# Attention and LoRA kernel: q and k by seven block products, and turned probabilities through device memory

## Chip, cores, metric

One core of one Trainium2 chip. The metric is the device time of one execution in microseconds; the time of a kernel is the median of its runs. TensorE multiplies, VectorE and ScalarE work on tiles in SBUF and PSUM, GpSimd on tiles in SBUF, and SyncE issues most transfers.

## What is computed

Four batches of 512 tokens of width 256. A block of attention (16 heads of 128) with modulated layer norm before it, then a dense layer with 8 LoRA experts, of which each token takes two:

```python
h = layernorm(x) * (1 + ca) + sa
q = h @ (wq_codes * repeat(wq_scales, 32)) + bq      # 256 -> 2048; k and v alike
scores = einsum('bqhd,bkhd->bhqk', q, k) / sqrt(128)
attn = softmax(scores)
out = einsum('bhqk,bkhd->bqhd', attn, v)
x = x + ga * (out @ wo + bo)
h = layernorm(x) * (1 + cb) + sb
x = x + gb * (h @ W.T + lora(h))                     # top 2 of 8 experts
```

All of it is in 32 bits. Each product is made of three matmuls on values split in a high and a low part (hi x hi + hi x lo + lo x hi), so every operand needs a `_hi` and a `_lo` tile: one engine rounds the value, another subtracts (`three`).

## The kernel before

The 2048 features are worked off in 8 pairs of heads (`pair(p)`; the first and the last are written out, the six between are a hardware loop). A pair has 8 steps, s = 0 to 7: one head of one batch, two heads of batch 0, then batch 1, 2, 3. The step's number is n = 8p + s. Every engine has its own program, and the engines meet by counting semaphores; the order on each engine is written out by hand.

TensorE, in step n: scores of step n (4 tiles of 3 matmuls with 512 columns), the weighted values of step n-2 (`weighted`, 12 matmuls of 512), q of step n+1 and k of step n+1 (`project`, 6 of 512 each: two chunks of the input's 256 features), the output projection of step n-2 (`out_project`, 12 of 256), v for step n+1 (`project_v`, 12 of 256). 

VectorE, in step n: v_lo, four row maxima (`maximum`), four 32x32 block transposes of the probabilities (`turn`, into `pB`), the reciprocal of the sums (`inverse`), o_lo, q_lo, k_lo, four additions of the scaled output rows to `y_acc` (`y_add`).

ScalarE: v_hi, four exponentials, o_hi, q_hi, k_hi, four copies of the landed probabilities into `pT_hi` (`prob_high`); it also issues the loads of the next pair's weights in steps 0 to 3. GpSimd: four low parts `pT_lo` (`prob_low`), the products of weight codes and scales (`product`) and the split of weights (`parts`).

A block transpose only turns inside 32x32 blocks; the blocks themselves must change partition. SyncE does that with 16 SBUF to SBUF transfers of 64 KB a step, from `pB` to `pT32`, which wait for the step's fourth turn (`pB_ok`); ScalarE waits for all of them (`p_land`). Landing buffers alternate between even and odd steps; `turned(par, kt)` is the view of one, in pieces of 32 elements. The fourth turn of step n waits until GpSimd has made the low parts of step n-2 (`p_lo_ok`).

The score banks are four of the eight PSUM banks; q and v share one (`qv_ps`), k has another (`ky_ps`), and `y_ps` is a bank of its own and score bank 3. `y_zero` tells VectorE that rows of `y_acc` which held other data have been set to zero; before, GpSimd does that in step 5 of the first pair.

## Time and profile before

| | |
|---|---|
| runs | 774.70, 774.38, 774.34 us (median 774.38) |
| profiled execution, span from first to last instruction | 771.9 us |
| median of the runs less that span | 2.5 us |
| busy: TensorE, VectorE, ScalarE, GpSimd | 766.2, 650.9, 520.4, 481.1 us |
| instructions | 14746 |
| one step in the middle of the span | 11.06 us |

Engines are named PE (matmuls), PEld (their weight loads, beside them), DVE (VectorE), ACT (ScalarE), POOL (GpSimd), SP (SyncE). In a timeline the first number is the start, the second the duration; durations overlap the next start, so what an instruction adds to a row of its kind is the distance of the starts. L1203 is line 1203 of the kernel; helpers such as `three` stand for all who call them, so groups are told apart by their tiles. The profiled execution has no time of its own beside the span: what lies around the span is taken as the 2.5 us between it and the median.

### The profile page before, as it was taken

Reading aid. Unit: us, or ns where it says so; the run is one execution under the profiler, and the core shown is the slowest. Engines: PE = TensorE matmul, PEld = TensorE weight load, DVE = VectorE, ACT = ScalarE, POOL = GpSimd, SP = SyncE. Lnnn points to the kernel's source line nnn. Section 1 sums busy time; section 2 is a strip of 40 time slices with the busy share of each in tenths; the row PEclk is TensorE's granted clock in tenths of the full one; section 3 lists DMA queues with packets and bytes.
Section 4 is the critical chain, followed back from the end, with each engine's and each line's share of the span. In section 5 each row is a group of like instructions: output and inputs, shape, how many; then the busy total and the mean of one; then the engine's idle time right before and its main releaser. Section 6 shows DMA issues by size and latency. Waiting matters only on the chain.

```text
span 771.9 us, 14746 instructions
## 1 busy us (share of the span) xinstructions
PE 766.2 (99%) x4212; PEld 667.1 (86%) x4212; DVE 650.9 (84%) x1259; ACT 520.4 (67%) x1133; POOL 481.1 (62%) x452
## 2 busy tenths in 40 slices
PE   8999999999999999999999999999999999999998
PEld 7888888888888888888888888888888888888897
DVE  7899889888888888888888888888888888879876
ACT  4788666766667676767676667676767676766841
POOL 5488566647655575547656675656657476789632
PEclk9999999999999999999999999999999999999999
DMA  8354465544454345544455434443455334433202
GB/s 260 96 153 123 98 146 151 143 101 100 125 145 125 95 98 139 138 111 99 114 142 134 99 93 134 133 129 92 105 137 152 96 92 108 113 87 86 55 1 110
DMA packets 71118, 89.92 MB, mean 116 GB/s; under 512 B 19409, under 2 KB 36522, under 8 KB 71086
## 3 DMA queue, kind: packets, MB, share of 16 engines
q1 hardware_dynamic: 52368, 73.21, 37.0%
q10 hardware_dynamic: 18718, 16.32, 7.3%
q8 instruction: 15, 0.25, 0.1%
q14 instruction: 17, 0.14, 0.1%
HBM read 21.30 MB, written 2.11 MB: 30 GB/s over the span
## 4 chain that ended last, share of the span: by engine, by line
PE 98%; DVE 1%; ACT 0%; issue 0%; POOL 0%; POOLq 0%
PE score L1202 10%; PE score L1203 10%; PE score L1204 9%; PE qv L1202 8%; PE qv L1204 8%; PE qv L1203 8%; PE o L1202 7%; PE o L1203 7%; PE o L1204 7%; PE ky L1202 4%; PE ky L1203 4%; PE ky L1204 4%; PE y L1202 2%; PE y L1204 2%; PE y L1203 2%; PE score L1408 1%
## 5 line engine op out<-in xcount | busy, mean ns | idle before, releaser
L432 POOL TENSOR_TENSOR pT_lo<-pT,pT_hi 128x512 fp32r<-128x512 f32 x248 | 314.6, 1305 | 238.0 <-ACT pT_hi L614 237.9
L708 ACT ACTIVATE prob<-score,neg_max 128x512 f32<-128x512 f32 x256 | 172.7, 688 | 78.5 <-DVE neg_max L1027 78.3
L1027 DVE TENSOR_REDUCE neg_max<-score 128x1 f32<-128x512 f32 x256 | 160.0, 682 | 1.3 <-PE score L1204 1.2
L1040 DVE STREAM_TRANSPOSE pB<-prob 128x512 f32<-128x512 f32 x252 | 156.7, 678 | 0.0
L614 ACT ACTIVATE pT_hi<-pT 128x512 fp32r<-128x512 f32 x248 | 135.3, 620 | 0.1
L1202 PE MATMUL score<-k_hi,q_hi 128*128 128x512 f32 x256 | 101.2, 395 | 0.2 <-DVE q_lo L934 0.2
L1203 PE MATMUL score<-k_lo,q_hi 128*128 128x512 f32 x256 | 100.3, 392 | 0.0
L1204 PE MATMUL score<-k_hi,q_lo 128*128 128x512 f32 x256 | 99.6, 389 | 0.0
L1202 PE MATMUL o<-pT_hi,v_hi 128*128 128x512 f32 x248 | 96.6, 389 | 0.0
L1204 PE MATMUL o<-pT_hi,v_lo 128*128 128x512 f32 x248 | 96.5, 389 | 0.0
L1203 PE MATMUL o<-pT_lo,v_hi 128*128 128x512 f32 x248 | 96.5, 389 | 0.0
L940 DVE SCALAR_TENSOR_TENSOR q_lo<-qv,vecT,q_hi 128x512 fp32r<-128x512 f32 x63 | 47.2, 749 | 43.6 <-ACT q_hi L597 43.6
L945 DVE SCALAR_TENSOR_TENSOR k_lo<-ky,vecT,k_hi 128x512 fp32r<-128x512 f32 x63 | 47.2, 750 | 31.3 <-ACT k_hi L601 31.2
L597 ACT ACTIVATE q_hi<-qv,bias_now 128x512 fp32r<-128x512 f32 x63 | 43.5, 690 | 44.0 <-PE qv L1204 43.7
L1202 PE MATMUL qv<-wv_hi,hT_hi 128*128 128x256 f32 x252 | 71.6, 284 | 0.0
L1203 PE MATMUL qv<-wv_lo,hT_hi 128*128 128x256 f32 x252 | 71.3, 283 | 0.0
L1204 PE MATMUL qv<-wv_hi,hT_lo 128*128 128x256 f32 x252 | 71.3, 283 | 0.0
L601 ACT ACTIVATE k_hi<-ky,bias_now 128x512 fp32r<-128x512 f32 x63 | 43.4, 690 | 40.4 <-PE ky L1204 40.4
L609 ACT ACTIVATE o_hi<-o 128x512 fp32r<-128x512 f32 x63 | 37.7, 599 | 44.4 <-PE o L1204 42.3
L951 DVE TENSOR_TENSOR v_lo<-qv,v_hi 128x512 fp32r<-128x512 f32 x63 | 43.5, 691 | 25.5 <-ACT v_hi L605 25.3
L1204 PEld LDWEIGHTS score<-k_hi,q_lo 128*128 128x128 f32 x256 | 48.1, 188 | 10.5
L1202 PEld LDWEIGHTS score<-k_hi,q_hi 128*128 128x128 f32 x256 | 48.3, 189 | 8.8 <-issue 0.4
(302 smaller groups left out, 1835.4 us busy)
## 6 DMA issues: line engine op xcount, KB each, us to landing
pT<-pB SPq DMA_DIRECT2D x1008, 64.0 KB, 2.0
out_dram<-x_nat SPq DMA_DIRECT2D x8, 256.0 KB, 2.3
stage<-in_L_attn_wv_codes_dram ACTq DMA_DIRECT2D x7, 256.0 KB
stage<-in_L_attn_wv_scales_dram ACTq DMA_DIRECT2D x14, 128.0 KB
stage<-in_L_attn_wq_codes_dram ACTq DMA_DIRECT2D x7, 256.0 KB
...
stage<-in_L_attn_wk_codes_dram ACTq DMA_DIRECT2D x7, 256.0 KB
...
```

The lines of the kernel that those rows point to most:

```text
L432: pool.tensor_tensor(split(pT_lo, kt), turned(par, kt), split(pT_hi, kt).bitcast(f32), ALU.subtract).then_inc(p_lo_ok, 1)
L597: act.activation(q_hi[:, :], qv_ps[:, :], ACT.Identity, bias=bias_now[:, 0, j:j + 1]).then_inc(q_hi_ok, 1)
L614: act.activation(split(to, kt), turned(par, kt), ACT.Copy).then_inc(p_hi_ok, 1)
L708: act.activation(prob[:, i], score_ps[i][:, :], ACT.Exp, bias=neg_max[:, i:i + 1], accum_out=row_sum[:, s % 2, i:i + 1]).then_inc(exp_ok, 1)
L940: dve.scalar_tensor_tensor(out=q_lo[:, :], in0=qv_ps[:, :], scalar=bias[:, 0, head], in1=q_hi[:, :].bitcast(f32), op0=ALU.add, op1=ALU.sub ...
L945: dve.scalar_tensor_tensor(out=k_lo[:, :], in0=ky_ps[:, :], scalar=bias[:, 1, head], in1=k_hi[:, :].bitcast(f32), op0=ALU.add, op1=ALU.sub ...
L951: dve.tensor_tensor(v_lo[:, par, tiles], v_view(bank), v_hi[:, par, tiles].bitcast(f32), ALU.subtract).then_inc(v_lo_ok, 1)
L1027: dve.tensor_reduce(neg_max[:, i:i + 1], score_ps[i][:, :], AX.X, ALU.max, negate=True).then_inc(max_ok, 1)
L1040: dve.transpose(pB[:, s % 2, :, i].rearrange("p g k q -> p k g q"), prob[:, i].rearrange("p (k g q) -> p k g q", k=QT, g=G)).then_inc(pB_o ...
L1202: pe.matmul(dst, a_hi, b_hi, start=first, stop=False)
L1203: pe.matmul(dst, a_hi, b_lo, start=False, stop=False)
L1204: return pe.matmul(dst, a_lo, b_hi, start=False, stop=last)
```

## The change

For pairs 1 to 7, the q of two heads for two batches is a product of 2x2 blocks (heads by feature chunks) with 2x2 blocks (feature chunks by batches). It is made by the form with 7 products and 15 additions of blocks in place of 8 products; the same for k. Four steps with one set of products are a cycle (`cycle`), two cycles a pair; heads come in the order 0, 1, 1, 0 (`HEADS`). Sums of input blocks (T) are made once, in the first pair, into the memory of `x_nat`, `z` and `gb_row`, and x is loaded again in the last pair; sums of weight blocks (S) are made per pair by GpSimd (`block_sums`). With t = s mod 4, TensorE makes products 1 and 2 at t = 3 of the step before the cycle, 6, 7 and 4 at t = 0, 5 at t = 1, 3 at t = 2; ScalarE copies partial sums out or into other banks (`first_copied`, `sum_kept`), VectorE adds the last product to a kept sum (`mixed_sum`), ScalarE and GpSimd split that (`mixed_high`, `mixed_low`). The output projection stands behind v in each step after the first pair; v has a bank of its own (`v_ps`, score bank 3), and `y_ps` uses score bank 2.

The turned probabilities go out to device memory in 4 transfers of 256 KB and come back in 1 of 1 MB that waits for all four. GpSimd writes the low part over the landed value (`pT_lo` is the memory of `pT32`), so TensorE reads it in pieces, and the fourth turn waits for the weighted values of step n-2 (`o_mm`).

SyncE and GpSimd:

```diff
                     for a in range(G):
-                        for g in range(G):
-                            sp.dma_start(flat(pT32[32 * g:32 * (g + 1), par, a]),
-                                         flat(pB[32 * a:32 * (a + 1), par, g])).then_inc(p_land[par], 16)
+                        sp.dma_start(turned_dram[par].rearrange("g c a e -> a c g e")[a],
+                                     pB[32 * a:32 * (a + 1), par].rearrange("c g i k q -> c g (i k q)")).then_inc(p_out, 16)
+                    sp.wait_ge(p_out, 16 * G * (n + 1))
+                    sp.dma_start(pT32[:, par].rearrange("p a i k q -> p (a i k q)"),
+                                 turned_dram[par].rearrange("g c a e -> (g c) (a e)")).then_inc(p_land[par], 16)
+                    if last and s == 1:
+                        sp.wait_ge(product_mm["k"], products(5, cycle(p, 0) + 1))
+                        for b in range(B):
+                            load_x(b)
...
+            def block_sums(m, p):
+                w = w32[m]
+                a11, a12, a21, a22 = w[:, 0, 0:HD], w[:, 1, 0:HD], w[:, 0, HD:PW], w[:, 1, HD:PW]
+                pool.wait_ge(w_prod[m], p + 1)
+                pool.tensor_tensor(s_sum(m, 1), a21, a22, ALU.add).then_inc(s_summed, 1)
+                pool.tensor_tensor(s_sum(m, 3), a11, a21, ALU.subtract).then_inc(s_summed, 1)
+                pool.wait_ge(s_summed, summed(m, p, 2))
+                pool.tensor_tensor(s_sum(m, 2), s_sum(m, 1), a11, ALU.subtract).then_inc(s_summed, 1)
+                pool.wait_ge(s_summed, summed(m, p, 3))
+                pool.tensor_tensor(s_sum(m, 4), a12, s_sum(m, 2), ALU.subtract).then_inc(s_summed, 1)
+            def mixed_low(m, src, count):
+                pool.wait_ge(mix_hi, mixes(m, count))
+                hi, lo = {"q": (q_hi, q_lo), "k": (k_hi, k_lo)}[m]
+                pool.tensor_tensor(lo[:, :], src[m], hi[:, :].bitcast(f32), ALU.subtract).then_inc(mix_ok, 1)
             def prob_low(n, par, kts=range(QT)):
                 for kt in kts:
                     pool.wait_ge(p_hi_ok, QT * n + kt + 1)
-                    pool.tensor_tensor(split(pT_lo, kt), turned(par, kt), split(pT_hi, kt).bitcast(f32),
+                    pool.tensor_tensor(turned(par, kt, pT_lo), turned(par, kt), split(pT_hi, kt).bitcast(f32),
                                        ALU.subtract).then_inc(p_lo_ok, 1)
...
+            def first_pair():
...
+                    else:
+                        parts_s23("q", 1)
+                        parts_s23("k", 1)
+                        v_weights_low(0)
+                        parts_22("q", 1)
+                        parts_22("k", 1)
+                    if s:
+                        prob_low(s - 1, (s - 1) % 2)
+                parts_s1("q", 1)
+                parts_s1("k", 1)
+                pool.wait_ge(t_subbed, 8)
+                for i in range(2):
+                    t = (B - 1) * QT + 2 * i
+                    pool.memset(y_acc[:, t:t + 2], 0.0).then_inc(y_zero, 1)
+                for count, i in enumerate((1, 3, 2, 4)):
+                    input_mix_lo(1, i, 5 + count)
...
             def pair(p, last=False):
...
+                        if s == 3:
+                            add_gated_bo(0)
+                            add_gated_bo(1)
                         elif s == 4:
+                            gate(0)
+                            add_gated_bo(2)
+                        elif s == 5:
+                            inverse_std(B)
+                        elif s == 6:
+                            gate(1)
+                        else:
+                            add_gated_bo(3)
+                            times_gb(1)
+                            times_gb(2)
+                            times_gb(3)
```

ScalarE and VectorE:

```diff
+            def first_cycle_step(p, s):
+                n = SPP * p + s
+                made = cycle(p, s // 4) + 1
+                o_high(n - 1)
+                first_copied("q", made + 1)
+                first_copied("k", made + 1)
+                q_high(SPP + 2 * made + 1, 0, first_ps["q"])
+                k_high(SPP + 2 * made + 1, 0, first_ps["k"])
+                prob_and_v(p, s)
+            def prob_and_v(p, s):
+                n = SPP * p + s
+                nxt = (s + 1) % SPP
+                prob_high((s - 1) % 2, landed(p, s - 1), kts=range(2))
+                v_out(n + 2, batch_of(nxt) % 2, nxt % 2)
+                prob_high((s - 1) % 2, landed(p, s - 1), kts=range(2, QT))
...
+                    if t == 0:
+                        exps(n, s, range(3))
+                        for m in "qk":
+                            sum_kept(m, 6, u2, now)
+                        exps(n, s, range(3, QT))
+                        o_high(n - 1)
+                        for m in "qk":
+                            sum_kept(m, 7, u3, now)
+                        q_high(SPP + 2 * now, 1)
+                        k_high(SPP + 2 * now, 1)
+                        prob_and_v(p, s)
+                    elif t == 3:
+                        exps(n, s, range(QT))
+                        first_cycle_step(p, s)
+                    else:
+                        exps(n, s, range(QT))
+                        for m in "qk":
+                            mixed_high(m, u3 if t == 1 else u2, 2 * now - 2 + t)
+                        o_high(n - 1)
...
+                        prob_and_v(p, s)
...
+            def turn(p, s, i):
...
+                if i == QT - 1 and not (early and s < 2):
+                    dve.wait_ge(o_mm, n - 1)
...
+            def pair(p, last=False):
...
+                    for i in range(QT):
+                        maximum(n, i)
...
+                    if t == 1:
+                        for m in "qk":
+                            mixed_sum(m, u3, 5, "u3", now, head_at(p, s + 1))
+                    elif t == 2:
+                        for m in "qk":
+                            mixed_sum(m, u2, 3, "u2", now, head_at(p, s + 1))
+                    for i in range(QT):
+                        turn(p, s, i)
+                    inverse(n, s)
+                    if s == 0:
+                        bv_through_wo(p)
+                    o_low(n - 1)
+                    if t == 0:
+                        q_low(SPP + 2 * now, head_at(p, s + 1))
+                        k_low(SPP + 2 * now, head_at(p, s + 1))
+                    elif t == 3:
+                        q_low(SPP + 2 * now + 1, head_at(p, s + 1), first_ps["q"])
+                        k_low(SPP + 2 * now + 1, head_at(p, s + 1), first_ps["k"])
+                    y_add(n - 2, batch_of(s - 2), (s - 2) % 4, False)
+                    v_low(n + 2, batch_of(nxt) % 2, nxt % 2)
                     if last and s in (4, 6):
                         attended((s - 4) // 2)
-                    if last and s == 5:
+                    if last and s == 4:
                         statistics(0)
```

TensorE:

```diff
+            def scores(p, s, q_and_k):
...
+                        pe.wait_ge(exp_ok, QT * (n - 1) + i + 1)
+                        if i == 2 and not (first and s < 3):
+                            pe.wait_ge(y_ok, QT * (n - 2))
+                        if i == 3:
+                            pe.wait_ge(v_lo_ok, n + 1)
...
+            def pair(p, last=False):
...
+                    if t == 0:
+                        for m in "qk":
+                            pe.wait_ge(kept_ok[m], kept("copy", now))
...
+                            product(mix_ps[m], m, 6, b, False).then_inc(product_mm[m], 1)
+                        weighted_ready(p, s)
+                        weighted(n - 2, s % 2, batch_of(s - 2) % 2, j)
+                        for m in "qk":
+                            pe.wait_ge(kept_ok[m], kept("u2", now))
+                            product(mix_ps[m], m, 7, b, False).then_inc(product_mm[m], 1)
+                        next_v_tile(p, s, 0)
+                        for m, done in (("q", q_mm), ("k", k_mm)):
+                            pe.wait_ge(kept_ok[m], kept("u3", now))
...
+                            product(mix_ps[m], m, 4, b, False).then_inc(done, 1)
...
+                        next_v_tile(p, s, 1).then_inc(v_mm, 1)
+                        out_projection(p, s)
+                    elif t < 3:
+                        i = (5, 3)[t - 1]
+                        for m in "qk":
...
+                            product(mix_ps[m], m, i, b, t == 1).then_inc(product_mm[m], 1)
+                        weighted_ready(p, s)
+                        weighted(n - 2, s % 2, batch_of(s - 2) % 2, j)
...
+                        next_v(p, s)
+                        out_projection(p, s)
```

At t = 3 (`first_outputs`): weighted, product 1 of q and of k, the first v tile, product 2 of q and of k, the second v tile, the output projection.

## Rows read from the trace of the kernel before

**Rows 1.** The page of the whole execution: busy time, and the chain that ended last.
```profile
PE 766.2 (99%) x4212; PEld 667.1 (86%) x4212; DVE 650.9 (84%) x1259; ACT 520.4 (67%) x1133; POOL 481.1 (62%) x452
...
PE 98%; DVE 1%; ACT 0%; issue 0%; POOL 0%; POOLq 0%
```

**Rows 2.** Waits of TensorE: engine, line, releaser, us in total, times, longest.
```profile
PE score L1209 <- POOL ident L371: 1.5, 1, 1.5
```

**Rows 3.** Windows, one step: length; PE, PEld, DVE, ACT, POOL busy; PEclk, DMA, GB/s.
```profile
404.84:415.90 11.06, 11.06 (x62) 9.63 (x61) 9.18 (x18) 7.84 (x18) 7.55 (x7) 1.00 0.50 126
```

**Rows 4.** Timeline of TensorE, the same step: start, duration, instruction.
```profile
404.84 0.40 PE L1202 MATMUL score<-k_hi,q_hi 128*128 128x512 f32 x1
...
407.59 0.39 PE L1202 MATMUL o<-pT_hi,v_hi 128*128 128x512 f32 x1
...
413.03 0.28 PE L1202 MATMUL y<-wo_hi,o_hi 128*128 128x256 f32 x1
...
415.90 0.40 PE L1202 MATMUL score<-k_hi,q_hi 128*128 128x512 f32 x1
```

**Rows 5.** Timeline of VectorE, the same step.
```profile
405.97 0.69 DVE L951 TENSOR_TENSOR v_lo<-qv,v_hi 128x512 fp32r<-128x512 f32 x1 [0.76 <-ACT v_hi L605]
406.58 2.47 DVE L1027 TENSOR_REDUCE neg_max<-score 128x1 f32<-128x512 f32 x4
408.97 2.48 DVE L1040 STREAM_TRANSPOSE pB<-prob 128x512 f32<-128x512 f32 x4
...
411.43 0.66 DVE L956 TENSOR_TENSOR o_lo<-o,o_hi 128x512 fp32r<-128x512 f32 x1
...
413.95 0.75 DVE L945 SCALAR_TENSOR_TENSOR k_lo<-ky,vecT,k_hi 128x512 fp32r<-128x512 f32 x1 [0.61 <-ACT k_hi L601]
414.62 0.86 DVE L982 SCALAR_TENSOR_TENSOR y_acc<-y,inv_sum,y_acc 128x256 f32<-128x256 f32 x2
415.40 0.87 DVE L982 SCALAR_TENSOR_TENSOR y_acc<-score,inv_sum,y_acc 128x256 f32<-128x256 f32 x2
```

**Rows 6.** Timeline of ScalarE, the same step.
```profile
410.51 0.60 ACT L609 ACTIVATE o_hi<-o 128x512 fp32r<-128x512 f32 x1 [0.43 <-PE o L1204]
...
413.82 0.62 ACT L614 ACTIVATE pT_hi<-pT 128x512 fp32r<-128x512 f32 x1
```

**Rows 7.** Timeline of GpSimd, the same step.
```profile
414.51 5.04 POOL L432 TENSOR_TENSOR pT_lo<-pT,pT_hi 128x512 fp32r<-128x512 f32 x4 [3.51 <-ACT pT_hi L614]
```

**Rows 8.** Groups of GpSimd, whole span: busy us, mean ns of one | idle before.
```profile
L416 POOL TENSOR_TENSOR wo_lo<-stage,wo_hi 128x256 fp32r<-128x256 f32 x16 | 11.8, 739 | 1.3
...
L518 POOL MEMSET y_acc<- 128x512 f32 x2 | 1.0, 548 | 0.0
```

**Rows 9.** Timeline of VectorE, last pair, steps 5 and 6.
```profile
694.65 1.96 DVE L1011 TENSOR_TENSOR x_nat<-y_acc,x_nat 128x1024 f32<-128x1024 f32 x1
...
705.76 1.40 DVE L838 BATCH_NORM_STATS2 stats<-x_nat 128x6 f32<-128x256 f32 x4
...
707.86 0.68 DVE L951 TENSOR_TENSOR v_lo<-qv,v_hi 128x512 fp32r<-128x512 f32 x1
```

**Rows 10.** SyncE's issues, 426.7 to 437.8 us (ns min/median/max).
```profile
L353 SPq DMA_DIRECT2D pT<-pB x17: 507/590/592, 426.6 to 437.7; - x17
```

**Rows 11.** DMA issues, whole span and (last three) 95 to 103 us: median to landing.
```profile
out_dram<-x_nat SPq DMA_DIRECT2D x8, 256.0 KB, 2.3
...
pT<-pB SPq DMA_DIRECT2D x12, 64.0 KB, 4.6
...
hT<-gate_rows ACTq DMA_DIRECT2D x1, 512.0 KB, 5.0
...
gb_row<-gate_rows ACTq DMA_DIRECT2D x1, 512.0 KB, 6.9
```

**Rows 12.** Matmuls of line 1222, one form: ns min/median/max, first and last start.
```profile
L1222 PE MATMUL y<-gb_row,pB x4: 634/634/634, 4.1 to 5.4; 128*128 128x256 f32 x4
...
L1222 PE MATMUL score<-pB x4: 379/379/483, 11.6 to 12.3; 128*128 128x256 f32 x4
```

949 lines of the change are left out of this document (584 added, 365 removed).

## The prediction

> **What bounds the kernel now.** I read the page first: TensorE is busy 99% of the span, and the chain that ended last is 98% TensorE [rows 1]. Then the waits of TensorE: the longest is 1.5 us, before the first step [rows 2]. So nothing is won on another engine, and TensorE pays for every matmul. I then took one step from the middle (step = one head of one batch; 64 of them). It lasts 415.90 - 404.84 = 11.06 us, at the full granted clock of 1.00 (2.4 GHz) [rows 3, 4], and it is a plain sum of matmul spacings: score matmuls (407.59 - 404.84)/12 = 0.229 us, other 512-column matmuls (413.03 - 407.59)/24 = 0.227 us, 256-column ones 0.120 us (413.03 to 415.90 for 24) [rows 4]. Beside that, VectorE has 9.2 us of work in the step, ScalarE 7.8, GpSimd 7.6 [rows 3]. VectorE has under 2 us to spare: this is what the reader should keep in view.
>
> **What the change takes away.** In pairs 1 to 7, q and k for two heads and two batches (a cycle of four steps) come from 7 products of 3 matmuls instead of 8, for q and for k: 6 fewer 512-column matmuls a cycle, 14 cycles, 84 matmuls x 0.227 = **-19.0 us**. Pair 0 projects as before. The four steps are no longer equal. By position t = s mod 4, TensorE's work is scores 2.75, weighted 2.72, v 1.44, output 1.44, and products: 6 matmuls (1.36) at t = 1 and 2, 18 (4.08) at t = 0, 12 (2.72) at t = 3. So the steps want 12.43, 9.71, 9.71 and 11.07 us; only the two short ones are in danger.
>
> **The wait that this creates.** The output projection is now the last work of every step (it stood before v), and it waits for o_lo, which VectorE makes late in its round. Call the start of a step E. The first output bank is ready about 0.5 us before E, the second at E + 0.20. VectorE adds tiles at 0.39 each: the last two run from E + 0.26 to E + 1.04. Then, each by its spacing [rows 5]: v_lo 0.61 (405.97 to 406.58), four maxima 2.39, at t = 1 and 2 the two new sums (priced as k_lo, 0.67 each, the same kind of instruction with one operand in PSUM), four turns and the small reciprocal 2.46 (408.97 to 411.43), o_lo 0.67. That ends at E + 0.26 + 0.78 + 0.61 + 2.39 + 1.34 + 2.46 + 0.67 = E + 8.51. TensorE wants it at E + 2.75 + 1.36 + 2.72 + 1.44 = E + 8.27 and sees it 0.04 after the end: a wait of 0.28 us in each short step. It can't be made up, for output, additions and maxima form a ring. At t = 0 and 3, o_lo is ready at E + 8.4 (the last turn waits for the weighted product, E + 7.0, then o_hi 0.60 [rows 6]) and E + 7.2, wanted at E + 10.99 and E + 9.63. One short step of the last pair is costed below, so 27 x 0.28 = **+7.6 us**. VectorE otherwise gets as many instructions as before; the weight splits, GpSimd's two low parts of q and k (1.25 each: four in 5.04, [rows 7]) and ScalarE's six more copies a cycle fit: in a short step GpSimd has o or weight parts 1.4, two low parts 2.5 and four parts of the probabilities 5.0, 8.9 of 9.99 us, and mixed k_lo ends near E + 8.2, wanted at E + 9.99.
>
> **Into the cycles.** VectorE's first round of pair 1 (step 8) waits for y_zero, which GpSimd now sets after pair 0. ScalarE reaches the probabilities of step 6 at 9.8 us into step 7, behind k_hi; GpSimd's four low parts take 5.0 from 10.4 on, with a gap or none, and end at 4.4 us into step 8. Then come four weight parts of 128 columns (under the 0.74 that 256 take; as 0.45: 1.8) and two memsets, 1.1 [rows 8]: VectorE starts at about E + 7.3 in place of E + 1.65. Behind its first three maxima stand three exponentials (E + 10.0), behind them ScalarE's copy of product 6 (0.6), and product 7 waits for that copy: it starts at E + 10.6 in place of 6.8, and product 4, which waits for the copy of product 7, another 0.4 late. **+4.2**. In pair 0, VectorE gets 8 subtractions of inputs and GpSimd 8 low parts and block sums; two engines fill up in steps 3 to 7: **+0.8**, between 0 and 3.
>
> **The last pair.** Statistics of batch 0 now follow the residual sum in the same step 4; they were a step apart. The sum takes 1.96, the statistics 707.86 - 705.76 = 2.10 [rows 9]: 4.1 us go between v_lo and the maxima of step 5, a short one: o_lo at E + 12.6 in place of 8.5. That is 4.1 + 0.28 of wait, less the 0.3 that the statistics cost in the kernel before: **+4.1**. GpSimd gets 5.2 us more work after step 7 (bias row 3, one gate product more), and the statistics of the later batches slip by 1.6, of which TensorE's transposes feel about **+0.5**. Reloading x (2 MB on SP's queue, ahead of step 2's probabilities) **+0.5**.
>
> **The trip through device memory.** SP's queue issues 16 transfers a step at 0.59 each [rows 10], which alone would be more than a 9.7 us step; 5 issues are 3 us. But the trip is now two trips in a row. Out: four issues at about 0.5, the last lands 2.3 after its issue (as out_dram, the only 256 KB writes [rows 11]) = 3.9 us after the last turn; or, if the last lands as slowly as the old transfers did beside the gate_rows loads (4.6), 6.1 [rows 11]. Back: 1 MB; gate_rows loads of 2 x 512 KB landed in 5.0 and 6.9, the second issued 0.4 later, so 5.0 to 7.3. Together 9.0 to 13.5 us; I take 10.5, nearer the low end, because the loads of gate_rows had other traffic beside them. Wanted: from t = 1 to t = 2 the time is shortest. The last turn ends at E + 7.85; ScalarE would take the block 7.6 us into the next step, E + 17.6, 9.7 us later. A late block only delays ScalarE's copies and GpSimd's low parts at first: the last low part comes 5.65 us after the landing (a copy 0.62, then 1.25 each, with ScalarE's v copy between), and TensorE needs it at the fourth part of the weighted product, 4.79 us into the step after that. E + 9.99 + 9.99 + 4.79 - 5.65 is 11.2 us after the turn at E + 7.85, and up to there nothing is lost. Cost taken: 0; above 11.2 each us costs 14 us (once a cycle). A rule of the Trainium skill speaks against this edit: "DMA: Bandwidth & Descriptors", Anatomy of one DMA, says that most of a transfer's fixed 2 us is the wait until the last byte is confirmed, and longest when the target is HBM. Its fit (2.0 us and 436 GB/s) would make an estimate of 4.4 us each way, 8.8 for both: the sum stays the same by it, too. The trace's 2.3 us for writes of 256 KB bears the rule out.
>
> pT_lo, read by TensorE in pieces of 32 from the landing buffer, costs nothing in my sum: ScalarE reads the same pieces at 0.62 us [rows 6]. TensorE's own price is not in the trace; below, nothing can be won by it.
>
> **The sum.** -19.0 + 7.6 + 4.2 + 0.8 + 4.1 + 0.5 + 0.5 = -1.3. The profiled span of 771.9 becomes 770.6; the runs' median lies 2.5 above the span, so **773.1 us**. The range of this case alone, with 0.1 us either way in each short step and 0 to 3 in pair 0, is 769 to 778.
>
> **Rivals.**
> *The short steps don't wait* (faster): VectorE's round is 0.3 us shorter than I add up, since the two sums or the additions start earlier. Then 773.1 - 7.6 = 765.5. For it: the margin is 0.28 of 9.7; against: every spacing is measured.
> *The trip is late* (slower, deciding from 11.2 us on): at 12.5 us it is 14 x 1.3 = +18, 791 us. For it: transfers of the old kind took 4.6 beside the gate_rows loads [rows 11], and in two of a pair's steps weights load beside it. Against: the writes' 2.3.
> *The clock falls in the two waits of 4 us* (steps 8 and 61). The trace of before has no such wait and no lower clock. What slow matmuls cost, its first microseconds show: a form at 634 ns that later takes 379 [rows 12]. Two stretches of about 6 us so, 3 us lost in each: 779. By the Trainium skill, "TensorE: Matmul & The Clock Gate", Why this matters for your kernels, long idle gaps bring the half rate back; no run here shows one yet.
> *The reads in pieces cost* 10% of the 248 pT_lo matmuls: +5.6, 779, worked from their 0.227 us; nothing in the trace speaks for it.
>
> **Chances.** Forecast 0.44 (of it 0.17 faster, 0.17 within 0.2%, 0.10 slower), no waits in the short steps 0.24 (faster), late trip 0.17 (slower), clock 0.10 (0.02 same, 0.08 slower), pieces 0.05 (0.02 same, 0.03 slower). 0.2%, 1.5 us, is about what a measurement of this kernel can tell from no change. Faster 0.41, same 0.21, slower 0.38. The range holds the no-wait case with half a us of the one-time terms off, and two thirds of the late trip: 764 to 787.
>
> **What would show it.** Right: TensorE's busy sum lacks 84 matmuls; four steps of 12.4, 10.0, 10.0 and 11.1 us; a wait of output matmuls on o_lo of 0.3 us, 27 times; one wait of about 4 us of product 7 on ScalarE's copy in step 8, one on o_lo in step 61; ScalarE's pT_hi waits for no landing. Wrong: weighted matmuls that wait for pT_lo with ScalarE waiting for DMA before it (late trip), a PEclk below 9, o<-pT_lo matmuls spaced over 0.227.

## The result

| kernel | runs | median | ratio to before, 95% interval |
|---|---|---|---|
| before | 4, 773.75 to 774.70 us | 774.36 us | |
| changed | 4, 833.65 to 836.69 us | 834.82 us | 1.0785 [1.0768, 1.0803] |

60.5 us slower, where 1.3 us faster was forecast: 835 lies far above the range of 764 to 787. The profiled spans are 831.7 and 771.9 us, 59.8 apart.

**Page of the changed kernel: busy time, granted clock in 40 slices, bytes, chain that ended last.** It answers to [rows 1].
```profile
PE 781.5 (94%) x4128; PEld 656.5 (79%) x4128; DVE 659.3 (79%) x1267; ACT 560.0 (67%) x1226; POOL 625.3 (75%) x656
...
PEclk9899998999999999999999999999999999999999
...
HBM read 89.45 MB, written 68.17 MB: 190 GB/s over the span
...
PE 39%; DVE 20%; DMA 14%; issue 13%; POOL 9%; ACT 2%; SPq 1%; ACTq 1%; DVEq 0%; POOLq 0%
```

The 84 matmuls are gone (4128 for 4212), but TensorE is busy 15.3 us longer. Part of its matmuls ran at the half rate (see the clock, below); in number 2 of the experiments, where little did, it is busy 769.3 us, 12.2 less. It is no longer the chain: from 98% to 39%. Two transfers that stood in no chain before hold 14% of it. GpSimd's busy time rose by 144 us.

**Waits of the changed kernel, five taken from the whole list: engine, line, releaser; us in total, times, longest.** They answer to [rows 2], where TensorE had one wait of 1.5.
```profile
ACT pT_hi L804 <- DMA pT<-turned: 61.5, 26, 5.7
...
PE score L1546 <- DVE v_lo L1249: 31.7, 21, 3.3
...
PEld y L1546 <- DVE o_lo L1254: 7.2, 20, 1.8
DVE neg_max L1311 <- POOL y_acc L651: 5.6, 1, 5.6
PEld qv L1546 <- ACT u L813: 4.2, 1, 4.2
```

The last three are waits that the prediction names. The first two are not: ScalarE waited for landings 26 times, where none was forecast, and score matmuls waited for v_lo.

**Where the time went.** I took the start of every step (the first score matmul) in both traces. What was added: 0.7 us before the first step, 17.7 in pair 0 (89.0 to 106.7), 32.4 in pairs 1 to 6 (530.9 to 563.3), 6.8 in pair 7 up to step 63, 2.2 behind it; together 59.8. The 0.7 before the first step are not to be explained by the change: in the runs below, which change nothing there, that stretch took 17.1 to 19.2 us (17.2 before, 17.9 changed). Inside a pair the loss has a place. The first four rows below are the first cycle of pair 2 (steps 16 to 19), the other four its second cycle (20 to 23). The columns are those of [rows 3], where a step took 11.06.

**Windows of the changed kernel, pair 2, one step each.**
```profile
223.27:235.82 12.55, 12.55 (x68) 10.71 (x67) 10.04 (x21) 9.50 (x21) 7.96 (x10) 1.00 0.62 177
235.82:246.01 10.19, 10.11 (x56) 8.50 (x55) 9.11 (x19) 5.74 (x14) 8.27 (x8) 1.00 0.67 193
246.01:257.26 11.25, 10.31 (x57) 8.44 (x55) 9.10 (x18) 7.10 (x16) 8.86 (x8) 1.00 0.85 209
257.26:273.61 16.35, 13.04 (x63) 10.64 (x62) 9.30 (x18) 10.28 (x22) 9.20 (x8) 0.90 0.78 213
273.61:286.17 12.56, 12.56 (x69) 10.71 (x68) 9.20 (x18) 9.54 (x21) 11.41 (x17) 1.00 0.79 212
...
286.17:296.30 10.13, 10.05 (x57) 8.51 (x55) 9.06 (x18) 8.13 (x19) 10.05 (x10) 1.00 0.47 149
296.30:306.43 10.13, 10.05 (x56) 8.51 (x55) 9.05 (x18) 5.88 (x15) 7.69 (x8) 1.00 0.71 207
306.43:317.61 11.18, 11.18 (x63) 9.59 (x61) 8.98 (x18) 9.29 (x21) 9.66 (x14) 1.00 0.81 241
```

The second cycle is close to the forecast lengths (12.4, 10.0, 10.0, 11.1): 44.00 us against 44.24 before. In the first cycle steps 3 and 4 take 27.60 in place of 21.31. That cycle is the one in which ScalarE's queue loads the next pair's weights. So one cycle in two is undisturbed or nearly so (44.0 us in pairs 2 and 6, up to 0.7 more in pairs 3 to 5, at its first step), and the other is 3.9 to 6.3 us longer than 44.0 in pairs 2 to 6 (and more in pair 1, by its step 8).

**The two trips side by side, changed kernel.** SyncE's issues in a cycle without weight loads and in the one with them:
```profile
294.11 2.78 SPq L436 DMA_DIRECT2D turned<-pB  x4
300.04 0.34 SPq L439 DMA_DIRECT2D pT<-turned  x1
```
```profile
243.81 2.78 SPq L436 DMA_DIRECT2D turned<-pB  x4
250.82 0.34 SPq L439 DMA_DIRECT2D pT<-turned  x1
254.98 2.88 SPq L436 DMA_DIRECT2D turned<-pB  x4
262.98 0.34 SPq L439 DMA_DIRECT2D pT<-turned  x1
```

Undisturbed: the four out take 300.04 - 294.11 = 5.9 us (forecast 3.9 to 6.1) and the return lands a median 4.9 us after its issue (forecast 5.0 to 7.3): 10.8, forecast 10.5, allowed 11.2. The four issues stand 0.7 us apart (forecast 0.5), and a transfer out lands a median 4.0 us after its issue, where the forecast took 2.3 to 4.6. The prediction's estimate of 8.8 us by the Trainium skill ("DMA: Bandwidth & Descriptors", Anatomy of one DMA) is 2.0 us short of this; the page gives that fit for transfers issued from GpSimd, and these are issued by SyncE.

Beside the weight loads, in pair 2: 7.0 out (250.82 - 243.81), and ScalarE gets the block at 260.41, 9.6 us after the issue, 16.6 in all. 16.6 - 11.2 = 5.4 us too late; steps 3 and 4 lost 6.3. The same trip, behind the second step of a pair, takes 15.2 to 16.6 us in pairs 2 to 6, so it is 4.0 to 5.4 us late.

**Timeline of ScalarE, changed kernel, end of step 18 and on; then TensorE's weight load at the same place.**
```profile
254.06 0.60 ACT L799 ACTIVATE o_hi<-o 128x512 fp32r<-128x512 f32 x1 [0.75 <-PE o L1548]
260.41 0.63 ACT L804 ACTIVATE pT_hi<-pT 128x512 fp32r<-128x512 f32 x1 [5.75 <-DMA pT<-turned]
...
260.94 0.61 ACT L804 ACTIVATE pT_hi<-pT 128x512 fp32r<-128x512 f32 x1
...
261.46 0.58 ACT L795 ACTIVATE v_hi<-score 128x512 fp32r<-128x512 f32 x1
```
```profile
262.82 0.19 PEld L1546 LDWEIGHTS score<-k_hi,q_hi 128*128 128x128 f32 x1 [3.74 <-DVE v_lo L1249]
```

The reader is to follow this chain: landing, two copies of pT_hi, v_hi at 261.46, v_lo, which frees the fourth score bank, and only then the fourth score tile. The prediction looked past v_hi, to the low parts 5.65 us behind the landing.

**The clock.** After this stop the matmuls ran at the half rate for a while.

**Timeline of TensorE, changed kernel, the same step.**
```profile
265.27 0.63 PE L1548 MATMUL o<-pT_hi,v_lo 128*128 128x512 f32 x1
265.70 0.63 PE L1546 MATMUL o<-pT_hi,v_hi 128*128 128x512 f32 x1
...
267.97 0.39 PE L1546 MATMUL score<-hT_hi,wq_hi 128*128 128x512 f32 x1
268.20 0.40 PE L1547 MATMUL score<-hT_lo,wq_hi 128*128 128x512 f32 x1
```

Starts are 0.43 us apart (1.2 GHz) from 264.4 to 267.4 and 0.23 behind that (2.4 GHz). The engine had stood idle for 3.3 us before 262.82. The granted clock of the step is 0.90, and 0.981 over the whole span, against 1.000 before. A mean loss of 1.9% of 831.7 us is an estimated 16 us; by the granted clock of each step 1.8 of it lie before the first step, 3.4 in step 1, 1.7 in step 7, 3.5 in step 8, 1.7 each in steps 11, 19 and 60, and 0.6 at the end. Number 2 of the experiments loses 3.9 us in the same way, so some 12 us of what the trip costs are half clock. Not every stop did this: behind stops of 2.3 us in steps 43 and 51 the granted clock stayed at 1.00, in step 11, with one of 2.05 us, it was 0.89. By the Trainium skill ("TensorE: Matmul & The Clock Gate", Why this matters for your kernels) idle gaps bring the half rate back; this trace agrees, in the steps named; steps 43 and 51 show that not every stop does so.

### The profile page after: what moved, and what is told of

Its sections match the earlier page's. It is cut to its first block, busy times and chain, and to the rows that moved or that the text cites. A ratio compares the mean times of both kernels' runs of the same rounds, so it can differ in the third digit from the quotient of the medians.

```text
span 831.7 us, 14600 instructions
## 1 busy us (share of the span) xinstructions
PE 781.5 (94%) x4128; PEld 656.5 (79%) x4128; DVE 659.3 (79%) x1267; ACT 560.0 (67%) x1226; POOL 625.3 (75%) x656
## 2 busy tenths in 40 slices
DMA packets 68677, 158.01 MB, mean 190 GB/s; under 512 B 8390, under 2 KB 25511, under 8 KB 60583
## 4 chain that ended last, share of the span: by engine, by line
PE 39%; DVE 20%; DMA 14%; issue 13%; POOL 9%; ACT 2%; SPq 1%; ACTq 1%; DVEq 0%; POOLq 0%
DMA pT<-turned 8%; DMA turned<-pB 6%; PE score L1546 5%; DVE pB L1326 5%; PE score L1547 5%; PE score L1548 5%; POOL pT_parts L573 4%; DVE neg_max L1311 3%; PE o L1546 3%; PE o L1547 3%; PE o L1548 3%; DVE y_acc L1280 3%; DVE u L1237 2%; DVE v_lo L1249 2%; PE y L1546 1%
## 5 line engine op out<-in xcount | busy, mean ns | idle before, releaser
L573 POOL TENSOR_TENSOR pT_parts<-pT,pT_hi 128x512 fp32r<-128x512 f32 x248 | 317.8, 1315 | 119.5 <-ACT pT_hi L804 119.5
L804 ACT ACTIVATE pT_hi<-pT 128x512 fp32r<-128x512 f32 x248 | 141.3, 623 | 61.7 <-DMA pT<-turned 61.5
L1547 PE MATMUL o<-pT_parts,v_hi 128*128 128x512 f32 x248 | 100.6, 406 | 0.0
L1280 DVE SCALAR_TENSOR_TENSOR y_acc<-y,inv_sum,y_acc 128x256 f32<-128x256 f32 x120 | 52.4, 478 | 33.5 <-PE y L1548 33.4
L1546 PE MATMUL score<-wv_hi,hT_hi 128*128 128x256 f32 x252 | 71.8, 285 | 0.4 <-ACT prob L873 0.4
L1547 PE MATMUL score<-wv_lo,hT_hi 128*128 128x256 f32 x252 | 71.5, 284 | 0.0
L1548 PE MATMUL score<-wv_hi,hT_lo 128*128 128x256 f32 x252 | 71.5, 284 | 0.0
L1249 DVE TENSOR_TENSOR v_lo<-score,v_hi 128x512 fp32r<-128x512 f32 x63 | 43.0, 683 | 32.6 <-ACT v_hi L795 32.6
L1546 PEld LDWEIGHTS o<-pT_hi,v_hi 128*128 128x128 f32 x248 | 48.0, 194 | 15.4 <-POOL pT_parts L573 4.0
L1548 PEld LDWEIGHTS score<-k_hi,q_lo 128*128 128x128 f32 x256 | 48.5, 189 | 11.1
L1548 PEld LDWEIGHTS o<-pT_hi,v_lo 128*128 128x128 f32 x248 | 47.7, 192 | 10.8
L1547 PEld LDWEIGHTS o<-pT_parts,v_hi 128*128 128x128 f32 x248 | 47.7, 192 | 10.6
```

The source lines that it names most:

```text
L573: pool.tensor_tensor(turned(par, kt, pT_lo), turned(par, kt), split(pT_hi, kt).bitcast(f32), ALU.subtract).then_inc(p_lo_ok, 1)
L804: act.activation(split(to, kt), turned(par, kt), ACT.Copy).then_inc(p_hi_ok, 1)
L1249: dve.tensor_tensor(v_lo[:, par, tiles], v_view(bank), v_hi[:, par, tiles].bitcast(f32), ALU.subtract).then_inc(v_lo_ok, 1)
L1280: dve.scalar_tensor_tensor(out=rows, in0=y_view(t, banks), scalar=inv_sum[:, ring, t:t + 1], in1=rows, op0=ALU.mult, op1=ALU.add).then_inc ...
L1546: pe.matmul(dst, a_hi, b_hi, start=first, stop=False, skip_group_check=joins)
L1547: pe.matmul(dst, a_hi, b_lo, start=False, stop=False, skip_group_check=joins)
```

## Experiments

Two theories at the start. **Trip**: the loss is the trip through device memory where it meets the weight loads. **Products**: it is the seven products, with too much for VectorE and GpSimd. All kernels are told against the kernel before on the same chip (773.9 to 774.4 us); numbers 9 and 11 have four runs, the others two. "Direct" below is number 2.

**1. The weight loads made small.** Loads of pairs 1 to 7 fill 16 partitions only, and the products multiply by one; the weights are then not the reference's.
```diff
-                queue.dma_start(codes[m][:, :, :], rows[:, bass.ds(2 * p, 2), :]).then_inc(ld_w[m], 16)
+                queue.dma_start(codes[m][0:16, :, :], rows[0:16, bass.ds(2 * p, 2), :]).then_inc(ld_w[m], 16)
...
-                pool.tensor_tensor(w32[m][:, :, :], codes[m][:, :, :], scales[m][:, :, :], ALU.mult).then_inc(w_prod[m], 1)
+                by = scales[m][:, :, :] if isinstance(p, int) and p == 0 else ones[:, 0:1].to_broadcast([P, 2, PW])
+                pool.tensor_tensor(w32[m][:, :, :], codes[m][:, :, :], by, ALU.mult).then_inc(w_prod[m], 1)
```


> The changed kernel, but the weight loads of pairs 1 to 7 bring only 16 of 128 partitions, so about an eighth of the bytes, and the weight products of those pairs multiply the codes by one in place of the scales: the weights are not the reference's, all instructions and waits stay. Theory (the trip through device memory is late, and it is late where weights load beside it): steps 2 and 3 of pairs 1 to 6, 25.8 us together on average, fall to 10.1 + 11.2 = 21.3; 6 x 4.5 = 27 us, and some of pair 0's 17 us too: 798 to 808 us in all. The return transfer after step 1, 9.6 us there, lands in 5. Rival (GpSimd is too full, it does 30 percent more work than before, and its low parts hold TensorE up): nothing changes for it, 830 to 836 us.

Measured: 799.55 us, ratio 1.033 [1.026, 1.040]. Steps 3 and 4 of every middle pair are now 10.2 and 11.2 us, first cycle like the second. ScalarE's wait for landings fell from 61.5 us to 17.2.

**2. Seven products, direct transfers.** The 16 SBUF to SBUF transfers of the kernel before, everything else as changed.
```diff
-                    for a in range(G):
-                        sp.dma_start(turned_dram[par].rearrange("g c a e -> a c g e")[a], ...
-                    sp.wait_ge(p_out, 16 * G * (n + 1))
-                    sp.dma_start(pT32[:, par]..., turned_dram[par]...).then_inc(p_land[par], 16)
+                    for a in range(G):
+                        for g in range(G):
+                            sp.dma_start(flat(pT32[32 * g:32 * (g + 1), par, a]),
+                                         flat(pB[32 * a:32 * (a + 1), par, g])).then_inc(p_land[par], 16)
```


> The changed kernel with the 16 direct transfers from pB to pT32 in place of the trip; seven products and low parts in place stay. Theory (the trip is the main loss): most of the 60 us come back. SyncE then needs 16 x 0.63 + 0.9 = 11.0 us for each step, TensorE wants 10.1 in two of four, so the blocks land about 12 to 13 us after the turn, 1 to 2 us too late once or twice in a cycle: 780 to 795 us. Rival (the loss comes from GpSimd, from the first pair's extra work or from TensorE's reads in pieces): above 815 us. If SyncE were no limit at all: 773 us, my forecast of the changed kernel.

Measured: 795.96 us, ratio 1.028 [1.025, 1.031], 1 us above the expected range. The span is 793.5: of the 59.8 us, **38.2 are the trip** (831.7 - 793.5) and **21.6 are the rest** (793.5 - 771.9). Of the 38.2, 7.7 lie in pair 0, 26.2 in pairs 1 to 6 and 3.4 in pair 7; 0.8 lie before the first step, where there is no trip yet. The cycles now last 44.1 to 44.4 us, against 44.24 before: in the middle of the kernel the seven products bring next to nothing. That is in part the direct transfers' own limit, as expected: SyncE issues them without a break, 37 in 23.4 us around pair 2's last steps, which is 10.1 us for the 16 of a step and so as long as a short step, and ScalarE waits 25.1 us in all for landings. The undisturbed trip has cycles of 44.0. The 21.6 are 10.0 in pair 0, 6.2 in pairs 1 to 6, of which step 8 alone is 7.0 (18.1 for 11.06), 3.3 in pair 7 and 2.2 behind step 63.

**3. The trip alone.** The kernel before, eight products, with the change's four transfers out and one back.
```diff
-                        for g in range(G):
-                            sp.dma_start(flat(pT32[32 * g:32 * (g + 1), par, a]),
-                                         flat(pB[32 * a:32 * (a + 1), par, g])).then_inc(p_land[par], 16)
+                        sp.dma_start(turned_dram[par]...[a], pB[32 * a:32 * (a + 1), par]...).then_inc(p_out, 16)
+                    sp.wait_ge(p_out, 16 * G * (n + 1))
+                    sp.dma_start(pT32[:, par]..., turned_dram[par]...).then_inc(p_land[par], 16)
```


> The kernel before with one part of the change alone: 4 transfers out to device memory and 1 back in place of 16, everything else as before. In that kernel the landed block is wanted 13.5 us after the step's last turn. If the trip takes 10.9 us without weights beside it and 13 to 15 with them, as in the trace of the changed kernel, it is late by up to 1.5 us in the four steps of a pair that load weights, and more in pair 0, where x and the first weights load: 780 to 800 us. Rival (the trip costs nothing by itself and only the new order of v behind the landed copies, or the seven products, costs): 774 us. Rival (fewer issues on SyncE bring something): below 773 us.

Measured: 794.18 us, ratio 1.026 [1.021, 1.031], span 790.8, 18.9 over before. The trip also costs without the seven products, half as much: with steps of 11.06 the late block has 11.06 - 10.13 = 0.9 us more to come for each short step that it spans. In the middle pairs two to four steps of eight are 0.2 to 2 us longer, all from the third to the sixth, in or just behind the weight loads (12.67, 11.75 and 12.39 in pair 4). The clock stayed at 1.00. The two edits together lose more than the sum of both: 59.8 for 18.9 + 21.6. Of the 19.3 us above that sum, 11.0 lie in pairs 1 to 6.

**4. v before the landed copies.** If the path over v_hi is all that costs, ScalarE should make v_hi first.
```diff
-                prob_high((s - 1) % 2, landed(p, s - 1), kts=range(2))
                 v_out(n + 2, batch_of(nxt) % 2, nxt % 2)
-                prob_high((s - 1) % 2, landed(p, s - 1), kts=range(2, QT))
+                prob_high((s - 1) % 2, landed(p, s - 1))
```


> The changed kernel with one line moved: ScalarE makes v_hi before, not between, the copies of the landed probabilities, so v_lo, the row maxima and the fourth score tile no longer stand behind the landing. Theory (a late landing costs mostly through this queue on ScalarE): TensorE's waits on v_lo, 56 us in all with those of its weight loads, go; what is left is GpSimd's low parts coming late, which have about 1 us more slack: 810 to 822 us. Rival (the landing is needed as early by GpSimd and TensorE as by v): 830 to 836 us.

Measured: 832.51 us, ratio 1.076 [1.069, 1.081]: my 810 to 822 was wrong and its rival right. GpSimd's low parts, the next in the queue, take over: weighted matmuls now wait 16.3 us for them, in the changed kernel 1.1. So the place at which the late block stops TensorE doesn't matter; that it is late does.

**Waits, v first: what grew, and ScalarE's own wait for landings that shrank.** The changed kernel has 119.5 in the first.
```profile
POOL pT_parts L573 <- ACT pT_hi L804: 130.4, 56, 7.0
...
ACT pT_hi L804 <- DMA pT<-turned: 38.6, 15, 4.9
```

**5. Which part of the weight loads.** A scale load names each row of the scales 32 times, for 32 partitions. This kernel reads as many distinct rows of the code tensors (weights not the reference's).
```diff
-                    src = bass.AP(SCALES[m].tensor, start, [[D, NB], [0, BLK], [1, D]])
-                    queue.dma_start(scales[m][:, j], src).then_inc(ld_w[m], 16)
+                    rows_j = CODES[m].rearrange("(h p) d -> p h d", p=P)
+                    queue.dma_start(scales[m][:, j], rows_j[:, bass.ds(2 * p + j, 1), :]...).then_inc(ld_w[m], 16)
```


> The changed kernel, but the loads of the weights' scales (pairs 1 to 7) read as many distinct rows of the code tensors, in place of each scale row read for 32 partitions; bytes, pieces and destinations are the same, and the weights are not the reference's. If it is the repeated reads of few rows of device memory that hold up the trip beside the weight loads, the 4th step of each middle pair falls from 15-16 us to near 11.2 and the time to 800 to 815 us. If it is the bytes and pieces as such, nothing changes: 830 to 838 us.

Measured: 805.91 us, ratio 1.041 [1.038, 1.044]: 28.9 us of the changed kernel's loss are gone, with the same 158.01 MB moved. The 4th steps of the middle pairs are 11.5 to 13.0.

**The DMA view, issues and landing times: first the changed kernel at 244 to 261 us, then this kernel at 234 to 251, the same two trips of pair 2.**
```profile
turned<-pB SPq DMA_DIRECT2D x8, 256.0 KB, 4.6
pT<-turned SPq DMA_DIRECT2D x1, 1024.0 KB, 9.6
```
```profile
turned<-pB SPq DMA_DIRECT2D x8, 256.0 KB, 4.3
pT<-turned SPq DMA_DIRECT2D x2, 1024.0 KB, 4.9
```

The return that took 9.6 us takes 4.9 beside distinct reads. The way out still takes 6.3 to 7.7 us here in pair 2's steps with loads (5.9 undisturbed), which is why the 4th steps aren't all at 11.2. What remains open: the rows are of another tensor as well, so it was not tried whether the repetition or the tensor's place counts.

**6. The return in four parts,** each waiting for its own transfer out.
```diff
-                    sp.wait_ge(p_out, 16 * G * (n + 1))
-                    sp.dma_start(pT32[:, par]..., turned_dram[par]...).then_inc(p_land[par], 16)
+                    for a in range(G):
+                        sp.wait_ge(p_outs[a], ...)
+                        sp.dma_start(flat(pT32[:, par, a]), turned_dram[par]...[a]).then_inc(p_land[par], 16)
```


> The changed kernel with the return cut in four of 256 KB, each waiting for its own transfer out and arriving in its own quarter of the tile, all counted on one semaphore. If it is the series of out and back that costs (5.9 and 4.9 us undisturbed), the parts overlap, the trip falls to 8.5 to 9.5 us undisturbed and the 4th steps of the middle pairs from 15-16 us to 11 to 13: 800 to 818 us. If it is bytes moved beside the weight loads (the same here, and the four issues and waits more on SyncE), it stays: 825 to 840 us.

Measured: 808.98 and 821.02 us, median 815.0, ratio 1.053 [1.034, 1.071]. Within what was expected of the overlap, but its two runs are 12 us apart, so only the direction is shown. The profile is of the slower one. The last of the four issues back comes up to 3.4 to 3.6 us behind the first where no weights load, after 2.8 us for those out. The 4th steps are 11.9 to 15.4 us, expected 11 to 13.

**7. y_acc cleared earlier, statistics a step later,** with direct transfers. GpSimd clears y_acc at the end of its step 7, ahead of the low parts and the last weight parts; VectorE takes the first residual statistics at step 5 of the last pair.
```diff
                         parts_22("k", 1)
+                        pool.wait_ge(t_subbed, 8)
+                        for i in range(2):
+                            t = (B - 1) * QT + 2 * i
+                            pool.memset(y_acc[:, t:t + 2], 0.0).then_inc(y_zero, 1)
...
-                    if last and s == 4:
+                    if last and s == 5:
                         statistics(0)
```


> Seven products with the 16 direct transfers, with two placements changed: the two clearings of y_acc for the batch of step 7 stand at the end of GpSimd's step 7 in place of its later place behind the turned probabilities' low parts, and the first residual statistics of the last pair stand one step later, as in the kernel before. If the long steps 8 (18.1 us) and 60 (16.2 us) come from the place of these two items, they fall to 12.5 to 13.5 us each and the time goes from 796.0 to 785 to 790 us. If other work was late there too, one or both stay above 15 us and the time stays within 793 to 797 us.

Measured: 804.77 us, ratio 1.040 [1.036, 1.043], 8.8 us worse than direct: wrong. Step 8 went from 18.1 to 17.2 only, and steps 60, 61 and 62 from 16.2, 12.5 and 10.9 to 15.2, 18.3 and 13.8. Two waits stood behind the ones that I had removed.

**Waits of this kernel: 117 to 136 us (step 8), then 702 to 746 us.**
```profile
DVE ga_bo L1262 <- POOL stage L490: 4.7, 1, 4.7
```
```profile
POOL mv L473 <- DVE var_eps L1132: 11.1, 1, 11.1
PEld score L1544 <- POOL k_lo L561: 7.8, 1, 7.8
```

VectorE's bias additions through the output weights (`bv_through_wo`, before o_low) wait for GpSimd's product of pair 1's output weights, for GpSimd is behind after pair 0 (the wait of 4.7 us). And GpSimd's own q_lo and k_lo of step 61 queue behind its wait for the moved statistics.

**8. o_lo before the last turn,** with direct transfers, at t = 1 and 2.
```diff
+                    for i in range(QT - 1):
+                        turn(p, s, i)
+                    if t in (1, 2):
+                        o_low(n - 1)
+                    turn(p, s, QT - 1)
```


> Seven products with the 16 direct transfers, with o_low ahead of the last turn on VectorE in the steps with t = 1 and 2. The forecast's term says that the short steps are held by the output projection waiting for o_lo: then each short step (10.1 to 10.2 us) falls toward 9.9 to 9.98 and the cycles of 44.2 us by about 0.4 us, 16 times: 788 to 792 us. The rival: the last turn is as urgent, since the transfer hangs on it, and the short steps stay at 10.1 or the steps behind them grow by as much: 794 to 798 us.

Measured: 811.41 us, ratio 1.048 [1.045, 1.051]. The short steps fell by 0.1 us (10.1 to 10.2 us in number 2, 10.0 to 10.1 here; expected 9.9 to 9.98), so o_lo did hold them, but each 4th step grew by 1.3 us (11.4 to 12.7): the transfers, which wait for the last turn and so start some 0.6 us later, were as urgent. The rival's direction, and more than it said.

**9. All placements.** Direct transfers; y_acc as in 7; the bias additions behind v_low; VectorE's eight subtractions of inputs in pair 0 moved from before v_low into its idle gap before q_low; statistics as in 7 with GpSimd's inverse deviation behind its low parts.
```diff
-                    if s == 0:
-                        bv_through_wo(p)
                     o_low(n - 1)
...
                     v_low(n + 2, batch_of(nxt) % 2, nxt % 2)
+                    if s == 0:
+                        bv_through_wo(p)
...
                     if not early:
                         o_low(n - 1)
+                    if s == 3:
+                        dve.wait_ge(zin_ok, QT)
+                        dve.wait_ge(h_ev, DC * 2)
+                        input_mix(0, 1)
+                        input_mix(0, 3)
```


> Seven products with the 16 direct transfers, and four placements: y_acc cleared at the end of GpSimd's step 7; VectorE's bias additions through the output weights (one step after a pair's start) behind v_low in place of before o_low; VectorE's eight subtractions of the input mixes of pair 0 into the gap before q_low in place of between the additions and v_low; the first residual statistics at step 5 of the last pair, with GpSimd's inverse deviation behind its low parts. If the losses of pair 0 (steps 12.5, 13.4, 12.7, 15.2 where 11.1 to 11.4 stood), of step 8 and of steps 60 and 61 come from where these items stand, pair 0 loses 3 to 7 us less, step 8 is near 12.6 and steps 60 and 61 near 12.6 and 12.5: 778 to 785 us. If the loss in pair 0 is the amount of VectorE's and GpSimd's work and not its place, pair 0 stays near 99 us: 785 to 791 us.

Measured: 809.88 us, ratio 1.046 [1.044, 1.047]: wrong by 25 us. Pair 0 gained 2.9 us and step 8 is 12.6, as expected. But the second step of every pair rose from 10.2 to 12.0, since two additions now stand between v_low and its maxima, and take it 1.84 us from the first start to the maxima's (durations of 0.47 and 1.28). Step 62 took 17.0 (direct 11.0), and the stretch behind step 63 was 2.8 longer.

**10. The same with the trip and distinct rows** (weights not the reference's): the edits of numbers 9 and 5 made in the changed kernel.


> The four placements together with the change's trip through device memory, and the scale loads reading distinct rows of the codes (the weights are not the reference's). By the runs before, the trip then costs 805.9 - 796.0 = 10 us over the direct transfers; if half of that was the same misplaced work, it is 2 to 6 us above the run with the direct transfers; if the trip undisturbed gives its 0.17 us a cycle back and nothing else, it is 1 to 3 us below it.

Measured: 811.94 us, ratio 1.049 [1.047, 1.051], 2.1 over number 9, within the first expectation. The 4th steps of pairs 2 to 6 are 11.2, against 11.5 to 11.6.

**11. Placements in gaps.** Direct transfers; y_acc and the subtractions as in 9; the bias additions at the 4th step, in the gap before q_low; the last pair as in "direct".
```diff
+                    if last and s == 0:
+                        bv_through_wo(p)
                     o_low(n - 1)
+                    if s == 3 and not last:
+                        bv_through_wo(p)
```


> Seven products with the 16 direct transfers; y_acc cleared at the end of GpSimd's step 7, the input mixes' subtractions of pair 0 in the gap before q_low, and the bias additions through the output weights at the 4th step of pairs 1 to 6 in the same kind of gap (2.07 us long); the last pair as in the run with the direct transfers alone. Expected against that run's 796.0 us: pair 0 2.9 us shorter, step 8 5.5 us shorter, the step after it up to 2.8 us longer, the second steps of the pairs back from 11.97 to 10.2 and the 4th unchanged at 11.4: 789 to 792 us. If GpSimd's lateness after pair 0 comes out elsewhere, 794 to 798 us.

Measured: 787.98 us, ratio 1.019 [1.016, 1.022], the best version with seven products, 1 us below what was expected. It beats the changed kernel by 46.8 us and still loses 13.0 of span to before: 7.0 in pair 0, 0.7 before it, 0.7 in pairs 1 to 6, 2.4 in pair 7, 2.3 behind. Its cycles in pairs 2 to 6 are as long as in number 2. Pair 0 was 3.0 us shorter than in "direct", step 8 5.5, the step behind it 0.6 longer.

**12. Number 11 with the trip and distinct rows** (weights not the reference's): the edits of numbers 11 and 5 made in the changed kernel.


> The same placements with the trip through device memory, scale loads on distinct rows of the codes (weights not the reference's). Middle cycles 43.99 in place of 44.2 us give 3 us back, the steps around 60 cost 2 to 4 us more with the trip: within 3 us of the run with the direct transfers. If the trip holds up pair 0 as well (13.7 for 12.5 us in its second step), 2 to 5 us above it.

Measured: 802.7 us (800.02 and 805.38), ratio 1.037 [1.033, 1.041]: 14.7 over number 11, and wrong on both counts. Pair 0 takes 100.2 for 96.0 us, the 4th step of pairs 1 and 2 is 12.7 and 12.9, and step 60 is 19.1 for 15.3. So the trip had no reserve here with distinct rows either. In number 10, where the second steps of 12.0 us leave it more time, it cost 2.1 us. What made it late in number 12's steps was not taken apart.

## Why the prediction was wrong, step by step

**The step that failed: the cost of the trip, taken as 0.** "Together 9.0 to 13.5 us; I take 10.5 [...] up to there nothing is lost." The trip's length was right where nothing else was loading (10.8) and so was the mechanism of the rival "the trip is late", which had a chance of 0.17. But it took 15.2 to 16.6 us beside the weight loads, outside my 9.0 to 13.5 (its own terms give 8.9 to 13.4). Only one cycle in two is late, for my rival's every one, but by 4.0 to 5.4 us and not 1.3, and some of the stops halve the clock. The sum of it is 38.2 us of span (number 2). Numbers 1 and 5 show that it hangs on the weight loads: 35.3 us of the changed kernel's time go with small loads, 28.9 with distinct rows. A row that I had could have warned: the gate_rows loads, which name each row for 128 partitions, took 5.0 and 6.9 us for half the return's bytes [rows 11]; I read them as "other traffic beside them".

**"The last low part ... TensorE needs it at the fourth part of the weighted product".** The wrong path, but a harmless error: v_hi stands behind two copies of the same block on ScalarE and comes first (waits above). With v ahead the low parts hold TensorE with the same loss (number 4).

**-19.0 for 84 matmuls.** The matmuls went, but a cycle lasts 44.0 us undisturbed, not 43.48. In a short step scores start (288.95 - 286.17)/12 = 0.232 us apart for the 0.229 of [rows 4], weighted matmuls (293.09 - 290.31)/12 = 0.232 for 0.227, and the first output matmul behind the wait is followed after 0.22 in place of 0.12. In a cycle 48 scores make +0.13, 48 weighted +0.22, two such starts +0.2: 0.55 x 14 = 7.7 us that the sum lacks. The wider spacing isn't everywhere: the products of this step keep (290.31 - 288.95)/6 = 0.227, and 256-column matmuls 0.12. For the weighted ones see the reads in pieces, below; why scores are wider wasn't tried.

**Timeline of TensorE, changed kernel, step 21 (t = 1), the start of the five groups.**
```profile
286.17 0.40 PE L1546 MATMUL score<-k_hi,q_hi 128*128 128x512 f32 x1
...
288.95 0.39 PE L1546 MATMUL qv<-z_parts,wq_hi 128*128 128x512 f32 x1
...
290.31 0.39 PE L1546 MATMUL o<-pT_hi,v_hi 128*128 128x512 f32 x1
290.53 0.40 PE L1547 MATMUL o<-pT_parts,v_hi 128*128 128x512 f32 x1
290.77 0.39 PE L1548 MATMUL o<-pT_hi,v_lo 128*128 128x512 f32 x1
...
293.09 0.28 PE L1546 MATMUL score<-wv_hi,hT_hi 128*128 128x256 f32 x1
...
294.40 0.28 PE L1548 MATMUL score<-wv_hi,hT_lo 128*128 128x256 f32 x1
294.77 0.39 PE L1546 MATMUL y<-wo_hi,o_hi 128*128 128x256 f32 x1
294.99 0.28 PE L1547 MATMUL y<-wo_lo,o_hi 128*128 128x256 f32 x1
```

**+7.6, the output projection waits for o_lo.** Right in place and size: 294.77 - (294.40 + 0.12) = 0.25 us, forecast 0.28. The list of waits has 20 of them, 7.2 us in all, where I named 27. Number 8 bears the mechanism out (short steps 0.1 us shorter), and shows that this swap doesn't win it back. The rival "no waits in the short steps" is ruled out.

**+4.2, y_zero and product 7.** Right mechanism, and nearly the right size: VectorE waited 5.6 us for the cleared y_acc and product 7 4.2 for ScalarE's copy, at the places named. Direct, step 8 took 18.1 us for my 12.43 + 4.2 = 16.6; the granted clock of that step is 0.91, which is worth 1.6 us. The cause goes further than the two clearings: with them gone, the next wait of 4.7 us stands there (number 7).

**+0.8, pair 0 filling up.** Mis-sized, 10.0 with direct transfers and 17.7 with the trip. VectorE's subtractions take two inputs from SBUF. I had priced them inside the engines' idle time; beside a busy GpSimd each takes 1.2 to 1.8 us, and they stood between y_add and v_low, where v_lo is the last thing the fourth score tile waits for.

**Timeline of VectorE and then of GpSimd, number 11: subtractions beside a busy GpSimd and beside an idle one.**
```profile
84.33 1.18 DVE L1242 TENSOR_TENSOR z<-router_space,y_acc 128x512 f32<-128x512 f32 x1
85.43 1.78 DVE L1242 TENSOR_TENSOR z<-router_space 128x512 f32<-128x512 f32 x1
...
96.21 0.68 DVE L1242 TENSOR_TENSOR gb_row<-router_space,z 128x512 f32<-128x512 f32 x1
96.93 0.69 DVE L1242 TENSOR_TENSOR router_space<-y_acc,gb_row 128x512 f32<-128x512 f32 x1
```
```profile
83.66 3.00 POOL L565 TENSOR_TENSOR x_nat_parts<-x_nat,x_nat_parts 128x512 fp32r<-128x512 f32 x2
...
93.02 2.55 POOL L565 TENSOR_TENSOR x_nat_parts<-x_nat,x_nat_parts 128x512 fp32r<-128x512 f32 x2
97.65 0.61 POOL L530 TENSOR_TENSOR wq_hi<-stage,ones 128x256 fp32r<-128x256 f32 x1 [2.08 <-PE ky L1548]
```

GpSimd is at work until 86.66 and idle from 95.57 to 97.65. The two engines slow each other (3.00 for 2.55). The Trainium skill ("VectorE: DVE Perf Modes", Two Vector instructions with no wait between them) says that an instruction with two SBUF inputs reads one through an interface shared with GpSimd; the trace agrees. Moving the eight took 3.0 us off pair 0 (number 11); 7 remain, 2.6 of them in step 7, 1.8 in step 4 and 1.2 in step 1, which no run here took apart.

**+4.1, statistics behind the residual sum.** Too large: step 61, where I put it, took 12.5 for 9.99, and its wait for o_lo was 1.6 us, not 4. Step 60 took 16.2 with direct transfers for 12.43, for other reasons, which the sum lacks: the transposes of the LoRA and router weights now stand in step 60 (in step 59 before) and take 1.0 us, and the scores behind them wait 0.9 for ScalarE's copy of the result; 1.2 more is a wait for v_lo.

**+0.5 behind step 63, +0.5 for reloading x.** 2.2 us behind step 63, with the trip and direct alike; not taken apart. The reload of x stands ahead of step 58's transfers out, which then took 10.4 us to the return's issue in place of 5.9; ScalarE waited 3.8 us for that return, TensorE 2.8 for v_lo, and step 60 ran at a granted clock of 0.91. So it takes 19.3 us for 16.2 direct.

**SyncE's issues, then ScalarE's wait, changed kernel.**
```profile
715.89 2.19 SPq L417 DMA_DIRECT2D x_nat<-in_L_attn_x_dram  x4
718.75 1.81 SPq L436 DMA_DIRECT2D turned<-pB  x4
```
```profile
735.16 1.15 ACT L804 ACTIVATE pT_hi<-pT 128x512 fp32r<-128x512 f32 x2 [3.84 <-DMA pT<-turned]
```

**"The clock falls".** The rival was right, and not in two places only (the steps are named above): clock 0.981 changed, 0.995 direct, 1.00 with the trip alone. Each fall cost 1.6 to 1.8 us in its step, or twice that, for my 3.

**"The reads in pieces cost 10%".** Not 10%, but perhaps not nothing: weighted matmuls on the pieces have a mean of 399 ns beside 391 and 395 for the other two kinds in the same stretch, and 389 for all three before. The 12 weighted matmuls of an undisturbed step take 2.78 us in the changed kernel and in number 2, and 2.72 in the kernel before and in number 3, which have no reads in pieces: an estimate of 0.06 x 62 = 4 us. No run changed the reads alone, so that they are the cause isn't shown. The sign that I gave for it, a spacing over 0.227, was there.
